# Reordering the first stage of a two-layer transformer kernel: the second conditioned sum moves from GpSimd to VectorE, the expert pick behind it

## The chip, the cores and the metric

The kernel runs on one core of a Trainium2 chip. The metric is device time in microseconds of one launch; the median of 3 runs before is 1029.15 us (1024.9 to 1030.83). A core has five engines with instruction queues of their own: TensorE (PE; PEld are its weight loads), VectorE (DVE), ScalarE (ACT), GpSimd (POOL), and SyncE (SP), which here only issues DMAs. Each engine takes its instructions in order; semaphores tie them together.

## The reference, cut to what matters

x is [2, 1024, 256] in float32. The change touches only what happens before and inside the first attention:

```
masked_w = weight * mask                      # weight [8, 256, 256]
w_bot = einsum('bg,got->bot', cond_8, masked_w)   # one 256x256 matrix per batch
h = einsum('bnt,bot->bno', x, w_bot) + bias
q, k, v = h @ wq, h @ wk, h @ wv              # 2 heads of 128
q, k = rope(first half), kept second half
x = x + softmax(causal(q k^T / 128)) v @ wo
expert = argmax(cond_8)                       # used by the stage after the attention
```

Behind it come a layer of experts picked by `expert`, a routed mixture of 8 experts, and a second layer (two gated MLPs and a shared one, a gated recurrence, an adapted projection and a ternary MLP). They fill about four fifths of the time and are not changed.

## The kernel before

The 2048 tokens (both batches) are held transposed, 256 features as two slabs of 128 partitions, in four chunks of 512 tokens: chunks 0 and 1 are batch 0, chunks 2 and 3 batch 1. Numbers that must be exact to float32 are split: ACT makes a rounded `_hi` part, VectorE (or GpSimd) the remainder `_lo`, and TensorE does three matmuls for each product.

The conditioned matrix is not applied to x. It is folded into the weights of q, k and v: `cw` (batch 0, VectorE) and `half`/`half_mask` (batch 1, GpSimd) are the sums over g of eight staged slabs of `cond_w` times a scalar, and a mask; `fold` multiplies the sum with the weights `aqkv` in four units (m, a), `fold_hi` (ACT) and `fold_lo` (VectorE) split the result; `fold_bias` does the same for the bias, with 24 one-column matmuls before the fold. Then, for each chunk, `rotated(w, c)` makes keys and queries: `same` is the product of the rotated features, `same_in` (ACT) writes them to SBUF, `swap` is a group of four DMAs on SP's queue that exchanges the halves, `cosines` and `sines` (VectorE) multiply them with the tables `ropeC` and `ropeS`, `rope_1` (VectorE) and `rope_0` (GpSimd) add them, `kept` and `skip` handle the other half. `value_tiles` makes the values. `split_input(c)` is the splitting of x: `x0_hi` (ACT), `x0_lo` (VectorE).

`attention(c)` steps through 8 tiles (2 heads x 4 blocks of 128 queries): score `S`, `max`, `exp`, `recip`, `norm` (GpSimd), transposes `T`, `p_col`, product `PV`, `o_hi`, `o_lo`. `weave(main, side)` takes a step of `side` after each step of the attention; the side work of attention 0 is the rotation and values of chunk 1, that of attention 1 is the fold of batch 1 and chunk 2.

The order on every engine is written by `plan()`, which appends units to a list for each engine; nothing is reordered at run time. `pick0` finds the chosen expert of both batches in ten tiny instructions on VectorE; `ld_pack0` (GpSimd), at the end of attention 0, loads that expert's weights into the stage buffer, and so waits for `pick0`, `cw` and `half_mask`. The probabilities of tiles 1 to 3 live in the same stage buffer. PSUM has eight banks; the first stage uses all of them in turn. The order before is:

```
run(conditioned_half())            # GpSimd: half 1..7, half_mask
pick0, cw, scale_q, x0(0), fold_bias, fold(0)
rotated k0, rotated q0, values 0, wo_hi / wo_lo, x0(1), x0(2), x0(3)
attention 0 with [k1, q1, v1]; attention 1 with [fold(1), k2, q2, v2]
```

DMA issues at the start: ACT's queue has the vector `cond`, the mask, `aqkv`, the bias, `wo`; SP's queue has four loads of `cond_w` (512 KB each, slabs 2i and 2i+1), x of chunk 0, both whole tables, x of chunks 1 to 3, and small ones.

## Time and profile before

| | us |
|---|---|
| median of 3 runs | 1029.15 (1024.9 to 1030.83) |
| the profiled execution, its own time | 1029.05 |
| its span in the profile | 1027.8 |
| PE / PEld busy | 941.4 / 782.9 |
| DVE / ACT / POOL busy | 507.1 / 437.7 / 291.6 |
| mean granted TensorE clock | 0.972 of full speed |

The profile shows one execution. Times in it run from the start of the span. "Busy" is the time in which an engine executes; idle time is put down to what released the instruction after it. The busy time of an engine is a sum over stages with different limits, so for a change in one stage that stage's own rows are read.

### The profile page before, as it was taken

Reading aid. Unit: us, or ns where it says so; the run is one execution under the profiler, and the core shown is the slowest. Engines: PE = TensorE matmul, PEld = TensorE weight load, DVE = VectorE, ACT = ScalarE, POOL = GpSimd, SP = SyncE. Lnnn points to the kernel's source line nnn. Section 1 sums busy time; section 2 is a strip of 40 time slices with the busy share of each in tenths; the row PEclk is TensorE's granted clock in tenths of the full one; section 3 lists DMA queues with packets and bytes.
Section 4 is the critical chain, followed back from the end, with each engine's and each line's share of the span. In section 5 each row is a group of like instructions: output and inputs, shape, how many; then the busy total and the mean of one; then the engine's idle time right before and its main releaser. Section 6 shows DMA issues by size and latency. Waiting matters only on the chain.

```text
span 1027.8 us, 12997 instructions
## 1 busy us (share of the span) xinstructions
PE 941.4 (92%) x4816; PEld 782.9 (76%) x4816; DVE 507.1 (49%) x938; ACT 437.7 (43%) x820; POOL 291.6 (28%) x259
## 2 busy tenths in 40 slices
PE   3889999999778899998399999999999999999998
PEld 2657867777677799997287788888888888886786
DVE  6545353466536555554357633333333333588544
ACT  1555556423144355544134424334343343325675
POOL 8343221402054355545534004114032040000000
PEclk9999999999879899999699999999999999999999
DMA  7130001202134333332422200300203003000011
GB/s 256 31 114 21 21 1 62 73 22 83 54 100 114 113 114 114 119 105 91 173 80 60 107 16 1 123 1 15 109 1 123 0 1 123 1 1 1 1 41 42
DMA packets 21358, 67.46 MB, mean 66 GB/s; under 512 B 4464, under 2 KB 11888, under 8 KB 18992
## 3 DMA queue, kind: packets, MB, share of 16 engines
q1 hardware_dynamic: 15872, 38.82, 10.8%
q0 software_dynamic: 4704, 26.49, 8.9%
q10 hardware_dynamic: 720, 1.32, 0.3%
q8 instruction: 39, 0.64, 0.3%
q14 instruction: 23, 0.19, 0.1%
HBM read 55.09 MB, written 9.44 MB: 63 GB/s over the span
## 4 chain that ended last, share of the span: by engine, by line
PE 69%; DVE 16%; ACT 6%; issue 4%; DMA 3%; SPq 0%; DVEq 0%; POOL 0%; ACTq 0%; POOLq 0%
PE banks L880 14%; PE banks L882 14%; PE banks L881 14%; PE banks L1065 4%; PE banks L1066 4%; PE banks L1064 4%; PE banks L950 3%; PE banks L934 2%; PE banks L1114 1%; PE banks L1113 1%; PE banks L941 1%; PE banks L1100 1%; PE banks L1101 1%; DMA expert_output<-y_rows 1%; DVE hidden L1627 1%
## 5 line engine op out<-in xcount | busy, mean ns | idle before, releaser
L880 PE MATMUL banks<-input_hi,mlp_hi 128*128 128x512 f32 x384 | 154.4, 402 | 1.5 <-DVE input_lo L1663 1.5
L882 PE MATMUL banks<-input_hi,mlp_lo 128*128 128x512 f32 x384 | 153.5, 400 | 0.0
L881 PE MATMUL banks<-input_lo,mlp_hi 128*128 128x512 f32 x384 | 153.1, 399 | 0.0
L1880 POOL TENSOR_TENSOR mlp_lo<-weight_stage,mlp_hi 128x768 fp32r<-128x768 f32 x40 | 73.6, 1839 | 242.5 <-ACT mlp_hi L1302 242.5
L1317 ACT CAST hidden_hi<-hidden 128x512 fp32r<-128x512 f32 x96 | 59.6, 621 | 178.3 <-DVE hidden L1673 109.9
L1679 DVE TENSOR_TENSOR hidden_lo<-hidden,hidden_hi 128x512 fp32r<-128x512 f32 x96 | 66.5, 693 | 71.2 <-ACT hidden_hi L1317 71.2
L1673 DVE SCALAR_TENSOR_TENSOR hidden<-banks,L_expert_weight,gelu 128x512 f32<-128x512 f32 x64 | 48.0, 750 | 102.4 <-PE banks L882 102.1
L1850 POOL TENSOR_TENSOR ffn_w_lo<-weight_stage,ffn_w_hi 128x512 fp32r<-128x512 f32 x48 | 61.9, 1292 | 115.3 <-ACT ffn_w_hi L1264 115.3
L880 PE MATMUL banks<-expert_in_hi,ffn_w_hi 128*128 128x320 f32 x256 | 82.5, 322 | 8.7 <-DVE hidden L1627 5.2
L880 PEld LDWEIGHTS banks<-input_hi,mlp_hi 128*128 128x128 f32 x384 | 72.8, 190 | 18.6 <-issue 1.9
L882 PEld LDWEIGHTS banks<-input_hi,mlp_lo 128*128 128x128 f32 x384 | 72.9, 190 | 17.2
L881 PEld LDWEIGHTS banks<-input_lo,mlp_hi 128*128 128x128 f32 x384 | 73.2, 191 | 16.7
L1311 ACT ACTIVATE gelu<-banks 128x512 f32<-128x512 f32 x96 | 57.3, 597 | 65.3 <-PE banks L882 65.2
L881 PE MATMUL banks<-expert_in_lo,ffn_w_hi 128*128 128x320 f32 x256 | 80.6, 315 | 0.0
L882 PE MATMUL banks<-expert_in_hi,ffn_w_lo 128*128 128x320 f32 x256 | 80.4, 314 | 0.0
L1065 PE MATMUL banks<-hidden_lo,mlp_hi 128*128 128x512 f32 x192 | 75.3, 392 | 0.0
L1064 PE MATMUL banks<-hidden_hi,mlp_hi 128*128 128x512 f32 x192 | 75.1, 391 | 0.0
L1066 PE MATMUL banks<-hidden_hi,mlp_lo 128*128 128x512 f32 x192 | 75.1, 391 | 0.0
L880 PEld LDWEIGHTS banks<-expert_in_hi,ffn_w_hi 128*128 128x128 f32 x256 | 49.3, 193 | 11.9 <-DVE hidden L1627 6.6
L1283 ACT CAST expert_hidden_hi<-hidden 128x320 fp32r<-128x320 f32 x64 | 29.4, 460 | 57.2 <-DVE hidden L1627 57.2
L1632 DVE TENSOR_TENSOR expert_hidden_lo<-hidden,expert_hidden_hi 128x320 fp32r<-128x320 f32 x64 | 33.9, 529 | 34.0 <-ACT expert_hidden_hi L1283 34.0
L880 PE MATMUL banks<-ffn_w_hi,expert_hidden_hi 128*128 128x256 f32 x160 | 48.8, 305 | 1.6 <-DVE y_rows L1639 1.6
(294 smaller groups left out, 2115.9 us busy)
## 6 DMA issues: line engine op xcount, KB each, us to landing
weight_stage<-in_packF SPq DMA_DIRECT2D x8, 1536.0 KB, 6.9
weight_stage<-in_shared SPq DMA_DIRECT2D x2, 3072.0 KB, 10.7
expert_output<-y_rows SPq DMA_DIRECT2D x40, 128.0 KB, 2.7
weight_stage<-in_cond_w SPq DMA_DIRECT2D x4, 512.0 KB, 8.0
residual<-in_xT SPq DMA_DIRECT2D x4, 512.0 KB, 13.6
first_half_swapped<-first_half SPq DMA_DIRECT2D x32, 64.0 KB, 2.0
routed_input<-x_rows SPq DMA_DIRECT2D x16, 128.0 KB, 1.7
weight_stage<-in_ffn_w SPq DMA_DIRECT2D x2, 1024.0 KB, 8.9
```

The costliest lines, as they stand in the source:

```text
L880: pe.matmul(o, wh, dh, start=(i == 0), stop=False)
L881: pe.matmul(o, wh, dl, start=False, stop=False)
L882: last = pe.matmul(o, wl, dh, start=False, stop=(i == len(terms) - 1))
L1064: pe.matmul(o, dh[:, i, ms], hiD[r][:, :], start=first, stop=False)
L1065: pe.matmul(o, dh[:, i, ms], loD[r][:, :], start=False, stop=False)
L1066: last = pe.matmul(o, dl[:, i, ms], hiD[r][:, :], start=False, stop=final)
L1311: act.activation(gelu_t[n % 2][:, :], bank(("gu", *key, 0)), ACT.Gelu_apprx_tanh, bias=0.0).then_inc(done)
L1317: act.copy(hiD[n % 4][:, :], prod_t[n % 2][:, :]).then_inc(done)
L1673: dve.scalar_tensor_tensor(prod_t[m % 2][:, :], o, wsel[:, n // 3, n % 3:n % 3 + 1], gelu_t[m % 2][:, :], ALU.mult, ALU.mult).then_inc(done)
L1679: dve.tensor_tensor(loD[m % 4][:, :], prod_t[m % 2][:, :], f(hiD[m % 4][:, :]), ALU.subtract).then_inc(done)
L1850: pool.tensor_tensor(lo, src, f(hi), ALU.subtract).then_inc(done)
L1880: pool.tensor_tensor(wDl[s][:, qs], stage[:, qs], f(wDh[s][:, qs]), ALU.subtract).then_inc(done)
```

## The change

The plan of the first stage is another one. `cw` comes first on VectorE. `pick0` comes after the rotation of chunk 0. The sum of batch 1 moves from GpSimd to VectorE: one `tensor_scalar` and seven `scalar_tensor_tensor` (as `cw` has) in the slab order 6, 7, 0 to 5, two of them before the fold, four between the units of the fold, two and the mask behind. x of chunk 1 is split before the rotation, of chunk 2 and 3 inside attention 0 and 1. The first rotation has a hand-written order (both `same` before both `kept`, the sines after the values). The vector's DMA goes first on SP's queue, `aqkv` and the bias go first on ACT's, and the tables are loaded in two halves, each ahead of x of the next chunk. Only tile 3's `exp` still waits for the stage buffer to be free.

```diff
+HALF_ORDER = [6, 7, 0, 1, 2, 3, 4, 5]
-    def conditioned_half():
-        for g in range(1, G):
-            pool.append(("half", g))
+    def conditioned_half(first, end):
+        for g in HALF_ORDER[first:end]:
+            dve.append(("half", g))
             yield
-        pool.append(("half_mask",))
...
+    def later_input(c):
+        split_input(c)
+        yield
+
+    def first_rotated():
+        for w in ("k", "q"):
+            product("out", "same", w, 0)
+            act.append(("same_in", w, 0))
+            sp.append(("swap", w, 0))
+        for w in ("k", "q"):
+            product("out", "kept", w, 0)
+            act.append(("skip", w, 0))
+            dve.append(("cosines", w, 0))
+        run(value_tiles(0))
+        for w in ("k", "q"):
+            dve.append(("sines", w, 0))
+            dve.append(("rope_1", w, 0))
+            pool.append(("rope_0", w, 0))
...
-    run(conditioned_half())
-    dve.append(("pick0",))
     dve.append(("cw",))
     act.append(("scale_q",))
     split_input(0)
+    run(conditioned_half(0, 2))
     use("out", [(n,) for n in range(8)])
     product("out", "fold_bias")
     act.append(("bias_in",))
-    run(folded(0))
-    run(rotated("k", 0))
-    run(rotated("q", 0))
-    run(value_tiles(0))
+    run(weave(folded(0), conditioned_half(2, 6)))
+    split_input(1)
+    run(conditioned_half(6, G))
+    dve.append(("half_mask",))
+    first_rotated()
+    dve.append(("pick0",))
     act.append(("wo_hi",))
     pool.append(("wo_lo",))
-    for c in range(1, NCH):
-        split_input(c)
     share_banks(False)
-    run(weave(attention(0), chain(rotated("k", 1), rotated("q", 1), value_tiles(1)), every=1))
+    run(weave(attention(0), chain(rotated("k", 1), later_input(2), rotated("q", 1), value_tiles(1))))
...
-    run(weave(attention(1), chain(folded(1), rotated("k", 2), rotated("q", 2), value_tiles(2))))
+    run(weave(attention(1), chain(folded(1), rotated("k", 2), later_input(3), rotated("q", 2), value_tiles(2))))
...
-    term, cmask = sb("cond_term", [P, KD, D]), sb("cond_mask", [P, KD, D])
+    cmask = sb("cond_mask", [P, KD, D])
...
             elif kind == "fold":
                 b, m, a = key
+                pe.wait_ge(*ready("scale_q"))
...
     def scalar_program():
-        act.dma_start(cond ...)
-        act.dma_start(cmask[:, :, :], A["cond_mask"]).then_inc(ld["mask"], 16)
         act.dma_start(aqkv[:, :, :], A["attn_qkv"]).then_inc(ld["aqkv"], 16)
         act.dma_start(bias_c[:, :], A["cond_bias"]).then_inc(ld["bias"], 16)
+        act.dma_start(cmask[:, :, :], A["cond_mask"]).then_inc(ld["mask"], 16)
...
-                elif n:
-                    act.wait_ge(*ready("half_mask"))
+                elif n == 3:
+                    act.wait_ge(*ready("half", HALF_ORDER[1]))
                     act.wait_ge(*ready("cw"))
...
             if kind == "pick0":
-                dve.wait_ge(ld["cond"], 16)
...
             elif kind == "cw":
                 w = cwF[0][:, :, :]
+                dve.wait_ge(ld["cond"], 16)
...
+            elif kind == "half":
+                g, = key
+                w, n = cwF[1][:, :, :], HALF_ORDER.index(key[0])
+                if n == 0:
+                    dve.tensor_scalar(w, cond_stage[:, g, :, :], cond[:, 1, g:g + 1], None, ALU.mult).then_inc(done)
+                else:
+                    dve.wait_ge(*ready("half", HALF_ORDER[n - 1]))
+                    dve.scalar_tensor_tensor(w, cond_stage[:, g, :, :], cond[:, 1, g:g + 1], w, ALU.mult, ALU.add).then_inc(done)
+            elif kind == "half_mask":
+                dve.wait_ge(*ready("half", HALF_ORDER[-1]))
+                dve.tensor_tensor(cwF[1][:, :, :], cwF[1][:, :, :], cmask[:, :, :], ALU.mult).then_inc(done)
...
-                dve.wait_ge(ld["rope"], 32)
+                dve.wait_ge(ld["rope"], 32 * (c % CPB + 1))
...
-            if kind == "half":
-                if g == 1:
-                    pool.wait_ge(ld["cond"], 16)
-                    pool.tensor_scalar(w, cond_stage[:, 0, :, :], cond[:, 1, 0:1], 1.0, ALU.mult, ALU.mult)
-                step(pool.tensor_scalar(term[:, :, :], cond_stage[:, g, :, :], cond[:, 1, g:g + 1], 1.0, ALU.mult, ALU.mult))
-                step(pool.tensor_tensor(w, w, term[:, :, :], ALU.add))
-            elif kind == "half_mask":
-                pool.wait_ge(ld["mask"], 16)
-                pool.tensor_tensor(cwF[1][:, :, :], cwF[1][:, :, :], cmask[:, :, :], ALU.mult).then_inc(done)
...
     def sync_program():
+        sp.dma_start(cond ...)
         for i in range(4):
             sp.dma_start(cond_stage[:, 2 * i:2 * i + 2, :, :], A["cond_w"][:, 2 * i:2 * i + 2, :, :]).then_inc(ld[f"cw{i}"], 16)
         sp.dma_start(xT[:, :, sl(0)], A["xT"][:, :, sl(0)]).then_inc(ld["x0"], 16)
-        for dst, src in ((ropeC, "ropeC"), (ropeS, "ropeS")):
-            sp.dma_start(dst[:, :], A[src]).then_inc(ld["rope"], 16)
-        for c in range(1, NCH):
+        for c in range(CPB):
+            for dst, src in ((ropeC, "ropeC"), (ropeS, "ropeS")):
+                sp.dma_start(dst[:, sl(c)], A[src][:, sl(c)]).then_inc(ld["rope"], 16)
+            sp.dma_start(xT[:, :, sl(c + 1)], A["xT"][:, :, sl(c + 1)]).then_inc(ld[f"x{c + 1}"], 16)
+        for c in range(CPB + 1, NCH):
             sp.dma_start(xT[:, :, sl(c)], A["xT"][:, :, sl(c)]).then_inc(ld[f"x{c}"], 16)
```

## Rows read from the trace of the kernel before

**Rows 1.** The page: busy time of each engine, and TensorE in 40 slices.

```profile
PE 941.4 (92%) x4816; PEld 782.9 (76%) x4816; DVE 507.1 (49%) x938; ACT 437.7 (43%) x820; POOL 291.6 (28%) x259
...
PE   3889999999778899998399999999999999999998
```

**Rows 2.** Windows: stretch, length, busy time of each engine (instructions), clock, DMA share, GB/s.

```profile
18.10:22.70 4.60, 0.01 (x1) 0.01 (x1) 4.49 (x5) 0.23 (x2) 4.32 (x4) 1.00 0.59 186
...
41.70:45.50 3.80, 3.42 (x10) 2.67 (x11) 3.80 (x3) 0.51 (x1) 1.92 (x1) 0.62 0.02 4
```

**Rows 3.** The chain of waits, 0 to 60 us: start, length, what.

```profile
0.80 5.32 DMA conditioning<-in_cond
...
10.06 1.11 DVE rows_of_L_cond L1424
...
22.69 6.84 PE banks L904 x16
...
40.35 5.49 DVE input_lo L1439 x3
...
51.06 0.70 DVE times_sin L1457
```

**Rows 4.** Views by tile: durations in ns (shortest/median/longest), starts, shapes; DMA landing times.

```profile
L1433 DVE SCALAR_TENSOR_TENSOR cond_weight<-weight_stage,conditioning,cond_weight x7: 1058/1061/1644, 11.6 to 19.9; 128x512 f32<-128x512 f32 x7
...
DMA to landing us min/median/max: 5.1/8.0/10.3
...
L898 PEld LDWEIGHTS banks<-cond_bias,ery_key_value_weights x24: 287/333/333, 12.8 to 17.7; 128*128 128x128 f32 x24
...
L904 PEld LDWEIGHTS banks<-ery_key_value_weights,cond_weight x16: 190/190/337, 22.7 to 28.7; 128*128 128x128 f32 x16
```

**Rows 5.** DMA issues, 0 to 30 us: count, size, median us to landing.

```profile
weight_stage<-in_cond_w SPq DMA_DIRECT2D x4, 512.0 KB, 8.0
...
ery_key_value_weights<-in_attn_qkv ACTq DMA_DIRECT2D x1, 768.0 KB, 9.8
```

**Rows 6.** Timeline, 0 to 13 us: start, length, instruction, idle time before it.

```profile
0.81 2.04 SPq L1902 DMA_DIRECT2D weight_stage<-in_cond_w  x4
...
12.82 5.25 PE L898 MATMUL banks<-cond_bias,ery_key_value_weights 128*128 128x1 f32 x24 [12.82 <-DMA cond_bias<-in_cond_bias]
```

**Rows 7.** Timeline, 25 to 44 us: ACT, VectorE and GpSimd.

```profile
25.65 0.48 ACT L1152 CAST folded_hi<-banks 128x384 fp32r<-128x384 f32 x1 [7.31 <-PE banks L904]
...
35.72 0.69 DVE L1457 TENSOR_TENSOR times_sin<-first_half_swapped,rope_sin 128x512 f32<-128x512 f32 x1 [3.21 <-DMA first_half_swapped<-first_half]
...
37.23 1.65 DVE L1454 TENSOR_TENSOR times_cos<-first_half,rope_cos 128x512 f32<-128x512 f32 x1
...
39.63 1.77 POOL L1810 TENSOR_TENSOR queries<-times_cos,times_sin 64x512 f32<-64x512 f32 x1 [1.30 <-DVE times_sin L1457]
...
41.37 2.25 POOL L1801 TENSOR_TENSOR out_weights_lo<-out_weights,out_weights_hi 128x512 fp32r<-128x512 f32 x1
```

**Rows 8.** Timeline, 46 to 64 us, inside attention 0: ACT and VectorE.

```profile
46.43 0.68 ACT L1161 ACTIVATE first_half<-banks,folded_bias 128x512 f32<-128x512 f32 x1
...
54.07 0.68 ACT L1161 ACTIVATE first_half<-banks,folded_bias 128x512 f32<-128x512 f32 x1
...
58.86 0.69 DVE L1457 TENSOR_TENSOR times_sin<-first_half_swapped,rope_sin 128x512 f32<-128x512 f32 x1 [2.76 <-DMA first_half_swapped<-first_half]
...
63.67 0.69 DVE L1471 TENSOR_REDUCE softmax_stats<-banks 128x1 f32<-128x512 f32 x1 [2.28 <-PE banks L935]
```

**Rows 9.** Timeline, 92 to 96 us, inside attention 1: ACT and VectorE.

```profile
92.04 1.23 DVE L1489 TENSOR_TENSOR input_lo<-residual,input_hi 128x1024 fp32r<-128x1024 f32 x1 [1.12 <-ACT input_hi L1212]
...
92.18 0.69 ACT L1161 ACTIVATE first_half<-banks,folded_bias 128x512 f32<-128x512 f32 x1 [0.17 <-PE banks L882]
...
94.21 0.96 DVE L1471 TENSOR_REDUCE softmax_stats<-banks 128x1 f32<-128x768 f32 x1 [0.95 <-PE banks L935]
95.26 0.90 ACT L1188 ACTIVATE weight_stage<-banks,softmax_stats 128x768 f32<-128x768 f32 x1 [1.54 <-DVE softmax_stats L1471]
```

More of the change, by code:

```diff
@@ L622 @@
 UNSIGNALLED = {
-    "half", "first", "first_row", "place", "digits", "pick1_norm", "pick1_a", "pick1_b", "pick1_c", "pick1_d",
+    "first", "first_row", "place", "digits", "pick1_norm", "pick1_a", "pick1_b", "pick1_c", "pick1_d",
     "back_rows", "back_kept", "ld_pack0", "phase0", "gather", "ld_mlp", "fetch",
@@ L846, in program @@
     dve_step = nc.alloc_semaphore("dve_step")
-    pool_step = nc.alloc_semaphore("pool_step")
     def sl(c):
@@ L1121, in scalar_program @@
     def scalar_program():
-        act.dma_start(cond[:, :, :], A["cond_8"].rearrange("b g -> (b g)").rearrange("(a n) -> a n", a=1).broadcast_to((P, B * G)).rearrange("p (b g) -> p b g", b=B)).then_inc(ld["cond"], 16)
-        act.dma_start(cmask[:, :, :], A["cond_mask"]).then_inc(ld["mask"], 16)
         act.dma_start(aqkv[:, :, :], A["attn_qkv"]).then_inc(ld["aqkv"], 16)
         act.dma_start(bias_c[:, :], A["cond_bias"]).then_inc(ld["bias"], 16)
+        act.dma_start(cmask[:, :, :], A["cond_mask"]).then_inc(ld["mask"], 16)
         act.dma_start(woS[:, :, :], A["attn_wo"]).then_inc(ld["wo"], 16)
@@ L1762, in pool_program @@
     def pool_program():
-        steps = 0
-        def step(ins):
-            nonlocal steps
-            steps += 1
-            ins.then_inc(pool_step)
-            pool.wait_ge(pool_step, steps)
         for t, v in ((ident, 0.0), (ident16, 0.0), (causal, 0.0), (before, 1.0), (ones16, 1.0), (ones32, 1.0), (both_parts, 0.0), (lgb[0], 0.0), (lgb[1], 0.0)):
@@ L1785, in pool_program @@
             done = sem.get(signal(kind))
-            if kind == "half":
-                g, = key
-                w = cwF[1][:, :, :]
-                if g % 2 == 0 or g == 1:
-                    pool.wait_ge(ld[f"cw{g // 2}"], 16)
-                if g == 1:
-                    pool.wait_ge(ld["cond"], 16)
-                    pool.tensor_scalar(w, cond_stage[:, 0, :, :], cond[:, 1, 0:1], 1.0, ALU.mult, ALU.mult)
-                step(pool.tensor_scalar(term[:, :, :], cond_stage[:, g, :, :], cond[:, 1, g:g + 1], 1.0, ALU.mult, ALU.mult))
-                step(pool.tensor_tensor(w, w, term[:, :, :], ALU.add))
-            elif kind == "half_mask":
-                pool.wait_ge(ld["mask"], 16)
-                pool.tensor_tensor(cwF[1][:, :, :], cwF[1][:, :, :], cmask[:, :, :], ALU.mult).then_inc(done)
-            elif kind == "wo_lo":
+            if kind == "wo_lo":
                 pool.wait_ge(*ready("wo_hi"))
@@ L1900, in sync_program @@
     def sync_program():
+        sp.dma_start(cond[:, :, :], A["cond_8"].rearrange("b g -> (b g)").rearrange("(a n) -> a n", a=1).broadcast_to((P, B * G)).rearrange("p (b g) -> p b g", b=B)).then_inc(ld["cond"], 16)
         for i in range(4):
```

## The prediction

> **What bounds the kernel now.** The page comes first. TensorE is busy for 941.4 us of the 1027.8 us span, and its row of forty slices (25.7 us each) shows 3, 8, 8 and then nines: the first slices are the emptiest [rows 1]. So an edit at the start can pay, and what it moves into the fourth slice can lose but hardly gain. The windows view shows the hole: from 18.1 to 22.7 us TensorE is idle while VectorE is busy for 4.49 of 4.60 us [rows 2].
>
> The chain of waits says who holds the start. Read it downwards: the conditioning vector lands at 6.1 us; then VectorE works alone, the ten tiny instructions of `pick0` until 11.17 us and after them the eight steps and the mask of `cw`; at 22.69 comes the fold on TensorE; at 40.35 three `x0_lo` in a row; at 51.06 the sines of k1, which had waited for a swap [rows 3]. Everything behind is released step by step from there, so I take it that a microsecond gained at that swap and not given back by 100 us is a microsecond at the end. The other 900 us are not touched.
>
> The steps of `cw` (L1433) take 1.06 to 1.64 us, median 1.06 [rows 4]. In the same stretch GpSimd makes batch 1's sum from the same stage; I read the short value as what a step costs beside a quiet GpSimd.
>
> **The change, part by part.** The sum is made against the profiled execution, 1029.05 us (span 1027.8 and 1.25 around it), 0.1 us below the median of 1029.15.
>
> *Pick later, GpSimd silent: when is `cw` done?* VectorE now starts as soon as the vector and the first stage DMA are there. The four stage DMAs are issued from 0.81 us within 2.04 us, 0.5 each, and land 5.1 us (shortest) to 10.3 us (longest) after their issue [rows 4, 6]: at 5.9 and some 12.5 us, and evenly between (8.1, 10.3). The vector's DMA now stands before them on SP's queue, 0.5 at most: 6.3, 8.5, 10.7, 12.9. Each load feeds two steps of 1.09 (1.06 and the gap), less than the 2.2 between loads, so the DMAs set the pace and not VectorE. The last load gives two steps and the mask: 12.9 + 3 x 1.09 = 16.2 us, where it was 22.64. By steps alone it would be 6.4 + 0.5 + 8 x 1.09 = 15.6, the lower bound.
>
> *Can TensorE take it?* `fold_bias` stands before the fold in TensorE's order. It started at 12.82, released by the bias's landing, and ran 5.25 us, to 18.07 [rows 6]. The bias's load now has 256 KB of mask (and the vector) less in front of it on ACT's queue. That queue had brought 1.0 MB by 11.5 us (the 768 KB of weights land 9.8 us after an issue at 1.7 [rows 5]) in some 6.5 us; an estimate of 1.6 us for 256 KB: start 11.2, end 16.4 us. The fold then starts at 16.4. If the queue gains nothing, at 18.1, the other bound. The new wait on `scale_q` is met, since `fold_bias` waits for the same.
>
> *VectorE from there to the rotation.* Before, the fold's first result was taken by ACT 2.96 us after the fold's start (25.65 against 22.69) in 0.48 us [rows 3, 7], and the fold's 16 matmuls took 6.84 us [rows 3], of which the last three quarters came 1.3 us a unit. Now, in VectorE's order: `x0_lo` 0 (1.23, as its like at 92.04 [rows 9]) to 17.4; half 6 (0.5) and half 7 (1.09) to 19.0; `fold_lo` 1 waits for ACT until 19.9 and ends 20.5. Then a half and a `fold_lo` alternate, 1.09 + 0.56 = 1.65 a pair against TensorE's 1.3: `fold_lo` ends at 22.1, 23.8 and 25.45, the last half between them at 26.5. Then `x0_lo` 1 27.75, two halves 29.95, mask 31.0, two cosines 32.45, sines k 33.2, `rope_1` k 33.9. Sines q meet GpSimd's `rope_0` k and take 1.65, as the cosines of q did at 37.23 beside that instruction [rows 7], to 35.55; `rope_1` q to 36.3, `rope_0` q (1.77) to 37.4. TensorE's four products (6 x 0.23 us each) and values (24 x 0.12) are done at about 32, and a swap needs 4.0 us from the end of `same_in` (47.11 to 51.06 [rows 3, 8]), for q from 27.0 to 31.0: both lie under VectorE's work. Of the 6.2 us won at the fold's start, the end of `rope_1` q keeps 40.3 - 36.3 = **4.0 us**. The eight added steps and the mask, 9.2 us, are largely paid by waiting that goes, 3.21 us for the swap alone [rows 7]. Were the added steps stretched to 1.64, 8 x 0.58 = 4.6 us more would go; nothing runs on GpSimd at that time, so I leave that out.
>
> *What follows on VectorE.* Before: three `x0_lo`, 5.49 us, ahead of the first maximum [rows 3]. Now: `pick0`. It took 4.95 us (6.22 to 11.17) beside a busy GpSimd. Its lower bound: at the 0.2 us of a `recip` or of any such tiny instruction with its gap, ten are 2.0 us. GpSimd has `rope_0` q until 37.4 and then `wo_lo` (2.25 [rows 7]) until 39.7, so most of `pick0` meets a busy neighbour: I take 4.1 us, nearer to the row, with 2.0 and 4.95 as bounds. The gain is 5.5 - 4.1 = **1.4 us**. The first maximum, the first `exp` and with it `same_in` of k1, on which the swap hangs (46.43 [rows 8]), come 5.4 us earlier. TensorE's product of k1 needs 3.5 us from the first score at a granted clock of 0.62, mostly the lower level of 1.2 GHz [rows 2], to 40.9: just in time.
>
> *`x0` 2 inside attention 0.* VectorE's `x0_lo` waits for ACT's `x0_hi` (1.04), which stands behind an `exp` that ended as `same_in` of q1 started, at 54.07. So 1.04 + 1.23, a maximum of 0.28, the next `exp` of 0.57 and gaps pass first: `same_in` of q1 comes 3.3 us later. Its sines come at 62.15 instead of 58.86, the maximum behind them at 63.7, and the next at 64.4 instead of 63.67, where VectorE had been idle for 2.28 us [rows 8]. TensorE's tiles and values don't wait for these sines. Of 3.3 us **0.7** are left. *`x0` 3 inside attention 1:* its `x0_lo` stands behind that of 92.04 and delays the maximum of 94.21 to 93.3 + 1.23 = 94.5, **0.3 us**; `same_in` of q2 moves from 92.18 behind the `exp` of 95.26, by 4.1 us, and its sines have until the next chunk's first score, some 10 us later, to be there [rows 9].
>
> *At nothing:* the tables in halves (two more issues on SP of some 0.75 each, long before the first swap at 25.6; the halves needed first are asked for earlier than the whole tables were); `ld_pack0`, released near 65 us and needing only things done by 41; the freed tile `cond_term`. If a load of x1 were late (needed at 23.9), each microsecond would go to the rotation.
>
> The sum: 1029.05 - 4.0 - 1.4 + 0.7 + 0.3 = 1024.65, so **1024.7 us**.
>
> **A rule weighed.** The row first: the 24 weight loads of `fold_bias` (L898) took 0.333 us in the median through all of its 5.25 us; those of the fold (L904), after a pause, range from 0.337 down to 0.190 [rows 4], so TensorE was at its slower level in the one and rose within the other. The Trainium skill, "TensorE: Matmul & The Clock Gate", "Part 1: The HAM clock gate", says that the array starts at half rate and gets the full one after sustained activity. By that rule a fold that follows `fold_bias` without a pause would be at the full rate sooner; by the row 5 us of `fold_bias` do not raise it. By the row the sum stays; by the rule the fold's first unit is 1.3 us shorter, but VectorE waits only 0.9 us for it, so 1023.8.
>
> **Rivals.**
> A. The bias lands no earlier, and `fold_bias` holds the fold until 18.1. For it: all queues share the same DMA engines. Against it: less stands in front. The first `fold_lo` waits till 21.6 instead of 19.9: 1.7 more, 1026.4 us.
> B. Slower than before: the `x0` pieces inside the attention chains are not absorbed. Place: VectorE and ACT between 54 and 98 us. Price: 3.3 + 4.1 = 7.4 us against a gain of 5.4: 1031.1 us. It decides from 5.4 us on. Against it: the idle time of 2.76 and 2.28 us on VectorE right behind [rows 8].
> C. Better than the sum: `pick0` in 2.0 us and the fold at full rate, 2.1 + 0.9 more: 1021.7 us.
> D. The change does nothing: VectorE is the bound from 20 to 36 us, and its added steps take 1.64 each, 4.6 us, leaving 1029.2.
>
> **How the numbers follow.** Forecast 0.56, A 0.14, B 0.07, C 0.14, D 0.09. A measurement of this kernel (three runs from 1024.9 to 1030.83) can hardly tell 0.5%, 5.1 us, from no change; the line lies at 1024.0. The forecast's own range is 1022.5 to 1027. The whole range takes in A, most of C and nearly D, and leaves B out: 1020.8 to 1029.0. Faster by over 0.5%: C and about half of the forecast's share, 0.41. Slower by over 0.5% (over 1034.3) needs B and more, 0.05. Same: 0.54.
>
> **What would show it.** Right: the mask of `cw` ends near 16.2 us, all steps at 1.06; the fold starts near 16.4; VectorE has no gap over 1 us from 20 to 36; `pick0` takes 3 to 5 us between 36 and 41; `same_in` k1 starts near 41; the sines of q1 have 3 to 4 us of waiting before them; from 110 us on TensorE is 4.4 us ahead of before. Wrong: steps of `cw` that wait for loads beyond 13 us, a fold that waits for `fold_bias` till 18 us, or a lead of 5 us at 41 that is gone at 110, which would be B. A granted clock that differs in later slices, which the edit doesn't touch, could hide or double a gain of this size.

## The result

The changed kernel takes 1022.63 us (median of 19 runs, 1020.65 to 1024.51) against 1027.69 us of the kernel before on the same chip (19 runs, 1024.36 to 1030.83). The ratio is 0.996 with a 95% interval of 0.9951 to 0.9969, so 4.1 us with an interval of 3.2 to 5.0; the two medians lie 5.1 us apart. Forecast were 1024.7 us, 4.4 us less than the profiled execution of before. 1022.63 lies inside the forecast's own range (1022.5 to 1027), at its lower edge; before itself came out 1.5 us lower than in the three runs that the forecast started from. By the ratio the gain is 0.4%, less than the 0.5% that the prediction drew as its line, and clear of no change at all.

The page of the changed kernel, its busy times and the row of forty slices, answers to [rows 1]:

```profile
PE 939.2 (92%) x4816; PEld 779.7 (76%) x4816; DVE 504.8 (49%) x947; ACT 437.3 (43%) x820; POOL 271.1 (27%) x243
...
PE   5799999999588899998399999999999999998998
```

The first slices read 5, 7, 9 instead of 3, 8, 8. GpSimd lost 20.5 us of busy time. VectorE got nine instructions more (947 against 938) and is busy 2.3 us *less*: eight sum steps and a mask were added to it and it still has less to do. So instructions of that stage became shorter. The views by tile show which, beside [rows 4]:

```profile
L1451 DVE SCALAR_TENSOR_TENSOR cond_weight<-weight_stage,conditioning,cond_weight x7: 751/752/752, 9.4 to 14.9; 128x512 f32<-128x512 f32 x7
L1461 DVE SCALAR_TENSOR_TENSOR cond_weight<-weight_stage,conditioning,cond_weight x5: 740/741/750, 18.0 to 24.8; 128x512 f32<-128x512 f32 x5
...
L1453 DVE TENSOR_TENSOR cond_weight<-cond_weight,cond_mask x1: 692/692/692, 15.7 to 15.7; 128x512 f32<-128x512 f32 x1
...
L923 PEld LDWEIGHTS banks<-ery_key_value_weights,cond_weight x16: 190/190/337, 16.5 to 23.0; 128*128 128x128 f32 x16
```

A step takes 0.74 to 0.75 us in every instance shown, where the prediction had read 1.06 us, the median of before, as the price beside a quiet GpSimd.

The issues of the first 30 us (issue to landing, median us) answer to [rows 5]:

```profile
weight_stage<-in_cond_w SPq DMA_DIRECT2D x4, 512.0 KB, 9.6
...
ery_key_value_weights<-in_attn_qkv ACTq DMA_DIRECT2D x1, 768.0 KB, 6.6
...
conditioning<-in_cond SPq DMA_DIRECT2D x1, 8.0 KB, 5.7
cond_bias<-in_cond_bias ACTq DMA_DIRECT2D x1, 1.0 KB, 7.8
```

The weights `aqkv` land 3.2 us sooner after their issue than before, and the stage's loads take longer beside them: median 9.6 us instead of 8.0.

The timeline from 8 to 21 us answers to [rows 6]:

```profile
8.87 0.49 DVE L1449 TENSOR_SCALAR cond_weight<-weight_stage,conditioning 128x512 f32<-128x512 f32 x1 [8.87 <-DMA weight_stage<-in_cond_w]
...
9.21 5.25 PE L916 MATMUL banks<-cond_bias,ery_key_value_weights 128*128 128x1 f32 x24 [9.21 <-DMA cond_bias<-in_cond_bias]
...
12.55 3.11 DVE L1451 SCALAR_TENSOR_TENSOR cond_weight<-weight_stage,conditioning,cond_weight 128x512 f32<-128x512 f32 x4 [0.38 <-DMA weight_stage<-in_cond_w]
...
16.54 4.04 PE L923 MATMUL banks<-ery_key_value_weights,cond_weight 128*128 128x384 f32 x6 [2.08 <-DVE cond_weight L1453]
...
19.99 0.56 DVE L1473 TENSOR_TENSOR folded_lo<-banks,folded_hi 128x384 fp32r<-128x384 f32 x1 [1.20 <-ACT folded_hi L1170]
```

`cw` ends at 16.39 us and the fold starts at 16.54, 6.15 us before its like in [rows 3]. `fold_bias` was done at 14.46, so it held nothing up.

The chain of waits from 32 to 49 us, for the chain of [rows 3]:

```profile
32.57 0.70 DVE times_sin L1486
33.37 0.69 DVE queries L1495
34.09 0.18 DVE tiny L1409
34.29 0.93 DVE tiny L1410
35.24 1.21 DVE tiny L1411
36.48 0.18 DVE tiny L1412
...
38.63 0.59 ACT first_half L1179
...
43.61 0.70 DVE times_sin L1486
...
46.72 0.94 ACT input_hi L1154
47.68 1.22 DVE input_lo L1468
```

`pick0` runs from 34.09 to 37.94: 3.85 us, of which two instructions take 0.92 and 1.20 us and most others 0.17. The last two rows are the moved `x0` 2: in attention 0 it stands in the chain itself. What was released when, in us before the like of [rows 3, 8] or of the same view of before:

| | before | changed | lead |
|---|---|---|---|
| fold starts | 22.69 | 16.54 | 6.15 |
| first score | 41.77 | 35.54 | 6.23 |
| `same_in` k1 | 46.43 | 38.53 | 7.90 |
| sines k1 | 51.06 | 43.61 | 7.45 |
| `same_in` q1 | 54.07 | 49.56 | 4.51 |
| sines q1 | 58.86 | 54.33 | 4.53 |
| first maximum of attention 1 (128x640) | 66.60 | 60.88 | 5.72 |
| first maximum of attention 2 | 109.94 | 105.02 | 4.92 |
| last but one residual add of that layer's attention | 183.91 | 179.03 | 4.88 |

The gain is made by 46 us, part of it is given back between 46 and 105 us, and the rest stays. The two spans differ by 7.1 us; the other 2.1 arise behind 461 us, where the lead was still 5.0. Between 500 and 600 us the granted clock is 0.91 in the one profile and 0.96 in the other. That is work that the edit doesn't touch, so I don't count these 2.1 us as its doing, though no run isolates them; the runs' 4.1 us are near 4.9 and not near 7.1.

Each column is one execution, and one execution is not the kernel. A second profile of the changed kernel (the run on a second chip, below) has leads of 5.69 at the first score, 6.23 at the sines of k1, 4.61 at the first maximum of attention 1 and 3.66 at the end of the stage, 1.2 us less than the first. One difference is TensorE's clock from 36 to 41 us, first profile, then second (columns as in [rows 2]):

```profile
36.00:41.00 5.00, 5.00 (x23) 3.36 (x22) 3.71 (x14) 2.79 (x8) 0.88 (x3) 1.00 0.07 16
```

```profile
36.00:41.00 5.00, 4.92 (x14) 3.85 (x15) 2.81 (x11) 1.15 (x3) 0.94 (x1) 0.50 0.01 3
```

The wait before it is the same (3.25 and 3.27 us for `rope_0`). Leads below that differ by about a microsecond are therefore not told apart.

### The profile page after: what moved, and what is told of

The parts are those of the page before. It is cut to its first block, busy times and chain, and to the rows that moved or that the text cites. A ratio compares the mean times of both kernels' runs of the same rounds, so it can differ in the third digit from the quotient of the medians.

```text
span 1020.7 us, 12989 instructions
## 1 busy us (share of the span) xinstructions
PE 939.2 (92%) x4816; PEld 779.7 (76%) x4816; DVE 504.8 (49%) x947; ACT 437.3 (43%) x820; POOL 271.1 (27%) x243
## 4 chain that ended last, share of the span: by engine, by line
PE 68%; DVE 16%; ACT 7%; issue 4%; DMA 4%; SPq 1%; DVEq 0%; ACTq 0%; POOL 0%; POOLq 0%
PE banks L898 14%; PE banks L900 13%; PE banks L899 13%; PE banks L1084 4%; PE banks L1083 4%; PE banks L1085 4%; PE banks L969 3%; PE banks L953 2%; PE banks L1133 1%; PE banks L1132 1%; PE banks L1119 1%; PE banks L1120 1%; PE banks L960 1%; DVE hidden L1656 1%; DMA expert_output<-y_rows 1%
## 6 DMA issues: line engine op xcount, KB each, us to landing
residual<-in_xT SPq DMA_DIRECT2D x4, 512.0 KB, 11.2
```

## The experiments

All kernels are edits of the changed kernel unless it is said, and compute the same. "Lead" is as in the table: how much earlier than in the profile of before the same instruction starts.

### The sum of batch 1 back on GpSimd

```diff
-            dve.append(("half", g))
+            pool.append(("half", g))
...
-    dve.append(("half_mask",))
+    pool.append(("half_mask",))
```

> The changed kernel with one part undone: batch 1's sum and mask are again on GpSimd (in slab order 0 to 7), everything else stays. Theory 1, a GpSimd that works on the same stage stretches VectorE's steps: the seven steps of cw go from 0.75 back to 1.06 to 1.64 us, cw's mask ends near 20.5 us instead of 16.4, the first score comes 2 to 4 us later than in the changed kernel though VectorE has 6.5 us less to do, and of the 4 to 5 us gained 1 to 3 are left (ratio to before 0.997 to 0.999). Theory 2, the gain comes from the order alone (pick behind, loads, first rotation): the steps lengthen but the time stays that of the changed kernel, ratio 0.996, since VectorE's queue is 6.5 us shorter.

Measured: 1027.6 us against 1027.56, ratio 0.9997 (0.9988 to 1.0006). The whole gain is gone, more than expected (0.997 to 0.999), though the loads, the late pick, the later inputs and the hand-made order are all still there. The view by tile:

```profile
L1452 DVE SCALAR_TENSOR_TENSOR cond_weight<-weight_stage,conditioning,cond_weight x7: 1053/1060/1641, 9.9 to 18.2; 128x512 f32<-128x512 f32 x7
L1450 DVE TENSOR_SCALAR cond_weight<-weight_stage,conditioning x1: 930/930/930, 9.0 to 9.0; 128x512 f32<-128x512 f32 x1
L1454 DVE TENSOR_TENSOR cond_weight<-cond_weight,cond_mask x1: 1634/1634/1634, 19.3 to 19.3; 128x512 f32<-128x512 f32 x1
```

Same instructions, same order, same data on VectorE up to the mask; only GpSimd's work beside them differs. Steps go from 0.75 to 1.06 and 1.64, the mask from 0.69 to 1.63, the first `tensor_scalar` from 0.49 to 0.93. The fold starts at 21.11 instead of 16.54, the lead at the first score is 0.56, and the attention stage ends 0.8 later than before.

The Trainium skill, "SBUF — State Buffer", section "Who interferes with whom", says that a VectorE instruction with two SBUF inputs contends with a GpSimd instruction that reads SBUF. The trace agrees (steps of 0.75 us against 1.06 to 1.64).

### The sum of batch 1 alone on VectorE

The kernel before, with only the sum moved (same slab order and places between the fold's units): `pick0` first, DMA order, inputs and rotation as before.

```diff
-    run(conditioned_half())
     dve.append(("pick0",))
     dve.append(("cw",))
...
+    run(conditioned_half(0, 2))
...
-    run(folded(0))
+    run(weave(folded(0), conditioned_half(2, 6)))
+    run(conditioned_half(6, G))
+    dve.append(("half_mask",))
```

> The kernel before with one part of the change alone: batch 1's sum on VectorE between the units of the fold (order 6, 7, 0 to 5). pick0 is first, the loads, the rotation of chunk 0 and all x0 pieces ahead of attention 0 are as before. Theory 1 (the sum's move carries the gain: steps of cw at 0.75 and not 1.06 to 1.64, pick0 in 2.1 and not 4.95 us): cw ends near 15 us, fold_bias still ends at 18.1 and the fold follows it, the three x0_lo take 3.7 and not 5.5 us, the lead is 4 to 5 us at the sines of k1 and is not lost inside the attentions: ratio 0.995 to 0.997, the whole of what the changed kernel gains. Theory 2 (the parts need each other): under 2 us, ratio above 0.998.

Measured: 1024.96 us against 1028.24, ratio 0.9963 (0.995 to 0.9976): as much as the whole change, within the measurement. From the timeline:

```profile
8.36 0.23 DVE L1446 TENSOR_SCALAR rows_of_L_cond<-tiny,partition_number 128x2 int32<-128x2 f32 x1
...
9.02 5.51 DVE L1456 SCALAR_TENSOR_TENSOR cond_weight<-weight_stage,conditioning,cond_weight 128x512 f32<-128x512 f32 x7
...
13.21 5.25 PE L919 MATMUL banks<-cond_bias,ery_key_value_weights 128*128 128x1 f32 x24 [13.21 <-DMA cond_bias<-in_cond_bias]
14.56 0.69 DVE L1458 TENSOR_TENSOR cond_weight<-cond_weight,cond_mask 128x512 f32<-128x512 f32 x1
...
18.32 2.27 PE L926 MATMUL banks<-ery_key_value_weights,cond_weight 128*128 128x384 f32 x3
```

`cw` is done at 15.25 us, although all ten instructions of `pick0` stand in front of it. But the fold starts only at 18.32, behind `fold_bias`, which had waited for the bias. The lead is 4.37 us there, 3.3 at the first score, and 3.05 at the end of the attention stage: hardly anything is given back on the way. I had expected a lead of 4 to 5 at the sines of k1, it is 3.26: the three `x0_lo` behind the rotation took 5.53 us, not the 3.7 that I gave them, because GpSimd's `rope_0` and `wo_lo` run beside them.

### The DMA order of before

```diff
+        act.dma_start(cond ...)
+        act.dma_start(cmask[:, :, :], A["cond_mask"]).then_inc(ld["mask"], 16)
         act.dma_start(aqkv[:, :, :], A["attn_qkv"]).then_inc(ld["aqkv"], 16)
         act.dma_start(bias_c[:, :], A["cond_bias"]).then_inc(ld["bias"], 16)
-        act.dma_start(cmask[:, :, :], A["cond_mask"]).then_inc(ld["mask"], 16)
```

and whole tables behind x of chunk 0 on SP's queue.

> The changed kernel with the DMA issues as before (vector and mask first on ACT's queue, whole tables, x of chunks 1 to 3 behind them). Theory 1, the loads' order matters through the bias: the stage loads land at 5.9, 8, 10.6 and 12.5 us, cw ends near 16 us as it does now, but the bias lands at 12.7 and fold_bias ends at 18.1, so the fold starts 1.5 us later and the end is 0.5 to 1.5 us slower. Theory 2, the order of the loads is without effect (the DMA engines carry the same bytes): fold at 16.5, same time within 0.4 us.

Measured: 1025.45 us, ratio 0.998 (0.997 to 0.9989), 1.7 to 2.1 us less gain than the changed kernel has (0.9963 and 0.996; only the second interval is clear of this one). Expected were 0.5 to 1.5. TensorE's timeline:

```profile
12.94 5.25 PE L916 MATMUL banks<-cond_bias,ery_key_value_weights 128*128 128x1 f32 x24 [12.94 <-DMA cond_bias<-in_cond_bias]
18.05 4.19 PE L923 MATMUL banks<-ery_key_value_weights,cond_weight 128*128 128x384 f32 x6
```

This is rival A of the prediction, made to happen: the bias lands 10.6 us after its issue, and `fold_bias` holds the fold until 18.05, while `cw` was done at 14.98. With the loads in the new order `fold_bias` is done at 14.46 and `cw` at 16.39: the second comes 1.4 us later, the first 3.7 earlier, and the fold 1.5 earlier. The leads at the end of the attention stage are 3.05 for the sum alone, 1.98 for sum and plan with the old loads, and 4.88 or 3.66 for everything. By them the loads' order is worth 1.7 to 2.9 us, which the times bear out, and the rest of the plan (pick, later inputs, hand-made rotation) costs 1.1; that is less than the 1.2 by which two executions of one kernel differ, so this cost is not shown.

### The pick first again

```diff
+    dve.append(("pick0",))
     dve.append(("cw",))
...
     first_rotated()
-    dve.append(("pick0",))
```

> The changed kernel with pick0 again ahead of cw on VectorE, all else kept. In the changed kernel VectorE waits for the first stage load until 8.87 us, and the vector lands near 6.5 us. Theory 1, moving the pick gained nothing and costs: beside a quiet GpSimd its ten instructions take about 2.1 us (0.2 each with gaps) and end before the first load, so cw still ends near 16.4; the 3.85 us that pick0 takes between the rotation and the first maximum go, but TensorE's product for k1 holds same_in of k1 at about 37.4 instead of 38.5, so 1 us is gained: about 1021.6, ratio 0.995. Theory 2, the pick had to go behind: it takes 4.95 us as before, cw starts 2.5 us later, and the kernel is 1 to 2.5 us slower than the changed one.

Measured: 1023.77 us, ratio 0.9953 (0.9939 to 0.9967); the changed kernel has 0.996. VectorE's timeline, two of the ten and what follows them:

```profile
6.84 0.17 DVE L1409 TENSOR_REDUCE tiny<-conditioning 128x2 f32<-128x16 f32 x1 [6.84 <-DMA conditioning<-in_cond]
...
8.70 0.23 DVE L1442 TENSOR_SCALAR rows_of_L_cond<-tiny,partition_number 128x2 int32<-128x2 f32 x1
9.13 0.49 DVE L1450 TENSOR_SCALAR cond_weight<-weight_stage,conditioning 128x512 f32<-128x512 f32 x1 [0.20 <-DMA weight_stage<-in_cond_w]
...
37.87 0.29 DVE L1501 TENSOR_REDUCE softmax_stats<-banks 128x1 f32<-128x128 f32 x1 [2.39 <-PE banks L954]
...
41.49 0.42 DVE L1501 TENSOR_REDUCE softmax_stats<-banks 128x1 f32<-128x256 f32 x1 [3.33 <-PE banks L954]
```

With GpSimd silent the ten take 2.1 us and end before the first load of the stage is there: ahead of `cw` they cost nothing. At 38 us nothing is gained by their absence in this execution, since VectorE then waits 2.39 and 3.33 us for TensorE, whose granted clock is 0.50 from 36.96 to 40.96. The microsecond that I had expected from it is not there: the lead at the end of the stage is 2.96, and by the times the two kernels can't be told apart.

### Both later inputs ahead of attention 0

```diff
     pool.append(("wo_lo",))
+    for c in (2, 3):
+        split_input(c)
```

and no `later_input` in the two attentions.

> The changed kernel with x of chunks 2 and 3 split ahead of attention 0 again (behind pick0), not inside attentions 0 and 1. Theory 1, the two pieces inside the attentions cost about 2.5 us of lead (7.4 us at the sines of k1, 4.9 us from 105 us on): ahead of the first maximum they cost 2.44 us once, the sines of k1 come 2.4 us later, and the end is the same within 0.5 us; the lead over before is then 5 us from 50 us on without a further loss. Theory 2, the pieces are absorbed inside the attentions and the loss of lead has another cause (the values, the banks): the end is 2 us or more slower than the changed kernel.

Measured: 1022.01 us, ratio 0.9939 (0.9926 to 0.9952). The two `x0_lo` take 2.35 us at 39.01 and the lead at the first maximum falls from 7.9 to 4.5. But then it stays: 4.42 at the sines of k1, 4.29 at those of q1, 4.28 at the 128x640 maximum, 4.11 at the end of the stage. In the changed kernel 2.5 us go between the sines of k1 and attention 2, in both of its profiles (7.45 to 4.92 and 6.23 to 3.78); here 0.3. So the two pieces are what costs the lead, as the first theory had it. As a measurement the two kernels can't be told apart: the intervals touch, and 4.11 lies between the changed kernel's 3.66 and 4.88.

### The changed kernel again, and the pick first with both inputs ahead

The first is the changed kernel itself on a second chip; the second has both edits above together.

> The changed kernel itself, once more, beside the following three on one chip, so that they are compared with it and not with an earlier chip. Ratio to before 0.995 to 0.997 in both theories. Its fold should again begin at TensorE's slower level; how many of its 16 matmul records take 0.64 us and not 0.32 differs between executions (5 before, 7 in the first profile of the changed kernel, 9 to 10 in later kernels), and the first score should move with it by 0.32 us a record.

> pick0 ahead of cw, and x of chunks 2 and 3 split ahead of attention 0. If the two edits add up (each was measured alone at 0.9953 and 0.9939 of before, the changed kernel at 0.996): x0_lo takes the place of pick0 ahead of the first maximum, beside a first score that is late anyway, and nothing is lost inside the attentions: ratio 0.993. If both bought the same microseconds: 0.994.

Measured on one chip (before: 1031.09 us): changed 1027.49, ratio 0.9963 (0.995 to 0.9976); with both edits 1023.18, ratio 0.9923 (0.9901 to 0.9944). The intervals don't meet. The changed kernel's second profile is the one compared above. On a third chip the second was run again:

> The kernel of e7 (pick0 ahead of cw, x of chunks 2 and 3 split ahead of attention 0) once more, beside the next two. Ratio to before 0.992 to 0.9945; a lead of about 6 us that stays the same from the sines of k1 to the last residual, since nothing is inserted into the attentions.

1021.96 us against 1028.24, ratio 0.9929 (0.9912 to 0.9946). VectorE's timeline of it:

```profile
34.68 0.69 DVE L1498 TENSOR_TENSOR queries<-times_cos,times_sin 64x512 f32<-64x512 f32 x1
35.84 3.95 DVE L1471 TENSOR_TENSOR input_lo<-residual,input_hi 128x1024 fp32r<-128x1024 f32 x2 [0.47 <-ACT input_hi L1156]
39.71 0.28 DVE L1503 TENSOR_REDUCE softmax_stats<-banks 128x1 f32<-128x128 f32 x1
40.69 0.42 DVE L1503 TENSOR_REDUCE softmax_stats<-banks 128x1 f32<-128x256 f32 x1 [0.70 <-PE banks L956]
```

The pair is now stretched to 3.95 us beside GpSimd, but it lies where VectorE would have waited for TensorE anyway (the 2.39 and 3.33 us of the run with the pick first). The lead is 6.05 us at `same_in` k1 and 5.97 at the end of the stage (in the other run 6.51 at the sines of k1 and 6.51 at the end): nothing is lost on the way. Of the edits measured beside the changed kernel on one chip, this is the only one that the times clear of it.

### Both inputs in the wait for the swap

The pick first; `x0_hi` 2 and 3 on ACT behind `wo_hi`; both `x0_lo` on VectorE (`extra`, for k1 alone) directly ahead of the sines of k1.

```diff
         dve.append(("cosines", w, c))
         yield
+        dve.extend(extra)
         dve.append(("sines", w, c))
```

> pick0 ahead of cw; x0_hi of chunks 2 and 3 on ACT behind wo_hi, where ACT stood idle for 4.6 us, and x0_lo of both on VectorE in front of the sines of k1, where it had waited 2.8 us for the swap. Theory 1 (the pieces cost what they delay in the queue): they are hidden, and the kernel is at 0.993 or below, not slower than e7. Theory 2 (VectorE is no longer late at that place since TensorE's slower clock holds the scores): no difference from e7 beyond 0.1%.

Measured: 1024.77 us, ratio 0.994 (0.9917 to 0.9962), with a lead of 4.12 at the sines of k1 and 3.75 at the end. The pair (2.34 us from 44.69) began only when the swap was landing (with the pick first and nothing there, these sines start at 45.32): the maximum ahead of it in VectorE's order had waited for TensorE until 44.14. The wait in which I had put it did not lie there any more: TensorE's clock was 0.50 from 36 to 41 us, and VectorE waited for scores instead. Its hiding was expected and did not happen. By the times alone it is not shown to be slower than the pair ahead (0.9923, the intervals overlap); the leads, 3.75 against 6.51, say so.

### TensorE kept busy

Matmuls of a constant that nothing reads are added: 40 ahead of `fold_bias`, 4 ahead of each group of it, 36 ahead of the fold.

```diff
+        def keep_busy(o, n):
+            for _ in range(n):
+                pe.matmul(o[:, 256:256 + P], ones16[:, :], ones16[:, :], start=True, stop=True)
```

> The changed kernel with matmuls of constants added that nothing reads (128 columns, bfloat16): 40 ahead of fold_bias, 4 ahead of each of its 6 column groups, 36 between it and the fold. Theory 1, TensorE's slower level holds the first stage now: with work before it the fold runs at 0.32 us a record from the start, 5.1 us instead of 7.3 to 8.2, the first fold_lo comes 1.3 us earlier and the first score 2 to 3 us earlier: 1 to 3 us faster than the changed kernel. Theory 2, VectorE's queue (halves, x0_lo) holds the stage: the fold gets shorter but the first score moves by under 0.7 us and the time stays within 0.5 us.

Measured: 1026.42 us, ratio 0.9958 (0.9943 to 0.9973), not to be told from the changed kernel beside it. TensorE's timeline:

```profile
9.38 0.38 PE L905 MATMUL banks<-ones_bf 128*128 128x128 bf16 x4 [1.34 <-DMA cond_bias<-in_cond_bias]
...
14.28 0.96 PE L922 MATMUL banks<-cond_bias,ery_key_value_weights 128*128 128x1 f32 x4
15.10 3.49 PE L905 MATMUL banks<-ones_bf 128*128 128x128 bf16 x36
18.43 3.77 PE L931 MATMUL banks<-ery_key_value_weights,cond_weight 128*128 128x384 f32 x11
```

The granted clock was 1.00 from 9 to 11 us and 0.51 from 11 to 15, so it fell to the lower level while TensorE ran `fold_bias` and the added groups. The 36 then took 3.49 us (at the upper level some 2.1, an estimate from 50 of them in 2.96 us in the next run), and held the fold until 18.43; its 16 loads then took 0.19 us each, with no slow start. What the faster fold gained, its later start ate. The run decides nothing on the size.

The next two add the same (16 instead of 36 ahead of the fold) and 50 more ahead of the first score, to the kernel with the pick first and both inputs ahead, and to the one with both inputs in the wait:

> The kernel of e10 with the unread matmuls of constants: 40 ahead of fold_bias, 4 in each of its groups, 16 (not 36) between it and the fold, and 50 ahead of the first score, where TensorE waits for the rotation. Theory 1 (TensorE's slower level holds both places): the fold starts at 16.5 us and takes 5.4 us instead of 7.3 to 8.2, the first score comes 1 to 2 us earlier; the products and scores behind it run at the full clock, which granted 0.50 from 36 to 41 us so far, but VectorE's x0_lo pair still stands ahead of the first maximum. 1 to 2 us faster than e10. Theory 2: VectorE's queue is as long as before and takes over at once: within 0.5 us of e10.

> The kernel of e8 (pick0 first, x0_hi of chunks 2 and 3 on ACT behind wo_hi, both x0_lo in front of the sines of k1) with the same unread matmuls. In e8 the swap had landed when VectorE reached the two x0_lo, since TensorE at its slower clock had delivered the scores 3.3 us late (maximum 1 at 41.2 us); so they stood in the way. Theory 1: with TensorE at the full clock max 1 comes near 37.5, VectorE reaches the pieces 3 us earlier and the swap's wait hides at least one of them: 2 to 3 us faster than e8 and not slower than e11. Theory 2: the swap itself comes earlier by as much, so the pieces stand in the way as before, and e12 stays 1 us or more behind e11.

Measured: 1021.68 us, ratio 0.9937 (0.9924 to 0.995), and 1019.95 us, ratio 0.9917 (0.9904 to 0.993), where the kernel of the first without the added matmuls had 0.9929 (0.9912 to 0.9946) on the same chip. The windows from 36 to 41 us, first of the inputs in the wait without them, then with them (columns as in [rows 2]):

```profile
36.00:41.00 5.00, 4.35 (x13) 3.37 (x13) 0.29 (x1) 1.71 (x4) 1.51 (x2) 0.50 0.02 3
```

```profile
36.00:41.00 5.00, 4.54 (x44) 3.89 (x42) 1.28 (x4) 3.09 (x7) 2.90 (x2) 1.00 0.02 3
```

The clock is 0.50, the lower level, behind 3.25 us of TensorE waiting for `rope_0`, and 1.00 when it is busy in that time. But it was 1.00 behind the same wait in the first profile of the changed kernel too; in all eleven other profiles without added matmuls ahead of the first score it was 0.50 to 0.64 in the 4 us from that score on. In the traces the busy TensorE is worth about 1.1 us with the inputs ahead (7.06 of lead against 5.97) and 1.6 with the inputs in the wait (5.32 against 3.75), about what separates the two profiles of the changed kernel (1.2). In the times the first shows nothing and the second 2.3 parts in a thousand, from different chips and with intervals that overlap. Of all kernels run the last has the best median, but it isn't shown to be better than the two runs at 0.9923 and 0.9929.

## Why the prediction was right, and where two errors met

The forecast's case came: VectorE done with `cw` near 16 us, part of the lead given back in the attentions, a net of 4 to 5 us. That GpSimd's silence lets VectorE finish `cw` and so starts everything earlier stands: the sum's move alone gives 0.9963, all without it 0.9997. Where the prediction looked for the gain it was in part wrong: it let VectorE start earlier by moving the pick and kept the steps at 1.06 us. The runs show the pick's move worth next to nothing once GpSimd is silent (`cw` ends at 16.85 us with the pick in front and at 16.39 and 16.70 with it behind), and the shorter steps carry it. The time agrees partly by luck, as the terms show. Point by point:

- **When is `cw` done.** Predicted 16.2 us, measured 16.39; fold at 16.4, measured 16.54. Both parts of the sum were off. The first load landed at 8.87 instead of 5.9 to 6.3 us (with `aqkv` first on the other queue; in the old order VectorE's first instruction on that load started at 6.23, released by the vector), and the pace of 2.2 us a load was not met either: the four loads land 7.5 to 10.6 us after their issues. Against that a step takes 0.75 and not 1.06 us, so two errors cancel and 16.2 is right by luck. Those of 1.06 in [rows 4] were already stretched by GpSimd. With 1.09 a step, the four behind the load of 12.55 and the mask would have ended at 18.0.
- **Can TensorE take it.** `fold_bias` from 11.2 to 16.4 predicted, measured 9.21 to 14.46. The order of the loads mattered more than the 256 KB that I counted: in the old order (from 12.94, with the fold at 18.05) it held the fold back. Rival A is the state that the new order avoids; it was priced at 1.7 us and measures 1.7 to 2.1.
- **VectorE from there.** `fold_lo` 1 at 19.9 predicted, 19.99 measured; the last part of the fold at 25.45, measured 24.91. The halves at 0.74 instead of 1.09, with the mask at 0.69, end this stretch at 28.9 instead of 31.0. The sines of q met only the last 0.1 us of `rope_0` k: they had waited 1.02 us for their swap, behind eight issues on SP's queue (0.59 us each in the median, 5.03 together), and took 0.69, not 1.65. The end of `rope_1` q was put at 36.3; it came at 34.06. This term, 4.0, measures 6.2.
- **`pick0`.** 4.1 us predicted, 3.85 measured; the gain 1.4, measured 1.7. But the gain is the absence of the three `x0_lo` there, not the place of the pick: with GpSimd silent the pick costs nothing ahead of `cw`. That `same_in` of k1 came 7.9 us earlier and not 5.4 is also TensorE's clock, 1.00 where the row of before had 0.62; in the second profile it is 0.50 and the lead 6.7.
- **`x0` 2 and 3.** `same_in` of q1 predicted 3.3 us later, measured 2.9 to 3.4 (a lead of 7.90 or 7.45 falls to 4.51). But of that 1.7 are left at the 128x640 maximum and not 0.7; the waiting before the sines of q1 was 0.94 us and not 3 to 4, since VectorE's other work was late as well. In attention 1 0.8 is lost and not 0.3 (0.8 in the second profile too). Together 2.5 instead of 1.0. Rival B has the right place and a third of its price (7.4).
- **The tables in halves and the two added issues.** Nothing waits for them in the trace, as said.
- **The clock.** The sum followed the row and not the rule weighed beside it. The trace agrees with the row: the fold followed `fold_bias` after 2.1 us, with loads at 0.34 until 20.2, and 7.28 us for its 16 matmuls against 6.84 before. Even a fold straight behind `fold_bias` (old DMA order, 18.05 us) had loads of 0.333 us in the median and took 8 us.

So the sum 4.0 + 1.4 - 0.7 - 0.3 = 4.4 measures 6.2 + 1.7 - 1.7 - 0.8 = 5.4 on the terms' places; the end of the stage shows 4.9 (0.5 goes between the first maximum, 7.9, and the sines of k1, 7.45, for which VectorE waits 2.80 us on the swap), and the runs show 4.1 (3.2 to 5.0). In the second profile the end of the stage shows 3.7. The result is closer than its terms: the gains were too small by 2.5 us and the losses by 1.5, which is luck. Of the signs that the prediction named, the steps of 1.06 us and the 3 to 4 us of waiting before the sines of q1 did not come.

## What to carry to other kernels

Before work is moved off a helper engine, look for the main engine's instruction in a stretch where the helper is silent: here the work taken over was more than paid for, since the helper had stretched each step from 0.75 to between 1.06 and 1.64 us. Small work that fits a wait for a load can stand there, even at the head of the critical queue; inside a chain of waits it can cost more than the idle time of the trace before suggests, because a shorter chain has less of it (here 2.5 us instead of 1.0). An order of loads is judged by what lands last for the next engine, and a small vector behind a large block can be that.

## What the runs showed of the hardware

VectorE's stretched instructions end just behind an instruction of GpSimd, even the smallest. Three of the ten of `pick0` and GpSimd's timeline in the changed kernel, then GpSimd in the kernel before:

```profile
34.29 0.92 DVE L1410 TENSOR_TENSOR tiny<-conditioning,tiny 128x16 f32<-128x16 f32 x1
35.24 1.20 DVE L1411 TENSOR_TENSOR tiny<-tiny,eight_minus_expert 128x16 f32<-128x16 f32 x1
36.48 0.17 DVE L1412 TENSOR_REDUCE tiny<-tiny 128x2 f32<-128x16 f32 x1
```

```profile
33.41 1.77 POOL L1818 TENSOR_TENSOR queries<-times_cos,times_sin 64x512 f32<-64x512 f32 x1 [0.73 <-DVE times_sin L1486]
35.14 1.27 POOL L1809 TENSOR_TENSOR out_weights_lo<-out_weights,out_weights_hi 128x512 fp32r<-128x512 f32 x1
```

```profile
9.88 1.26 POOL L1795 TENSOR_TENSOR cond_weight<-cond_weight,cond_term 128x512 f32<-128x512 f32 x1
```

A 128x16 `tensor_tensor` ends at 35.21, just behind GpSimd's end at 35.18; the next at 36.44, just behind 36.41; alone it takes 0.17. In the kernel before it is the same: the last of the ten, at 10.06 [rows 3], ends at 11.17, GpSimd's `tensor_tensor` at 11.14. A 128x512 `tensor_tensor` that begins inside a GpSimd instruction ends 0.53 to 0.56 us behind that one's end (the mask of `cw` before at 22.64 against 22.08, with the sum back on GpSimd at 20.95 against 20.42), where it takes 0.69 alone. The `tensor_reduce` at 34.09, with one input, took 0.17 beside the same GpSimd instruction. It goes both ways: `wo_lo` takes 1.27 us here and 2.25 beside the pair of `x0_lo`, which takes 3.96 instead of 2.35 (pick first and inputs ahead).

`fold_bias`, 24 matmuls of one column in 5.25 us, ran at TensorE's lower level: its loads take 0.333 us in the median in the trace of before, and those of the fold 0.34 and then 0.19. In the run with added matmuls a group of four of them takes 0.56 us at a granted clock of 1.00 and 0.96 us at 0.51, and the clock fell from the one to the other while they ran. The clock column reads 1.00 over `fold_bias` in the changed kernel (9.2 to 14.5 us), where its loads are as long as at the lower level, so for such matmuls the loads tell it and the column doesn't. How many of the fold's 16 loads are slow varied between executions, and with it its length: 7.28 and 7.5 us in the two profiles of the changed kernel, 7.8 and 8.3 in the two with the pick first and both inputs ahead, 6.84 before.

What stays open: whether keeping TensorE busy ahead of the first scores shortens the time. The traces show 1.1 to 1.6 us of lead, about as much as two executions of one kernel differ, and one pair of runs shows nothing. Why the clock behind the same wait was 1.00 in one profile of the changed kernel and 0.50 in the other is open too.
